# Attention's end of a four-layer graph network: its own order of work, softmax sums as a product, output norm regrouped

## The chip, the cores and the metric

One core of a Trainium2 chip runs the whole kernel. The metric is the device time of one execution in microseconds, as the median of several runs. Five engines work side by side and meet only at semaphores: TensorE (PE in the profile, with its weight loads as PEld), VectorE (DVE), ScalarE (ACT), GpSimd (POOL) and SyncE (SP), which here only issues DMAs. Each engine takes its own instructions strictly in order.

## What is computed

A stack of four graph layers over x, 16 x 512 nodes x 128 features, each followed by a residual and a layer norm. Only the last layer and its norm matter here:

```python
# layer 3, per image; h = 4 heads of 32, E = 256 edges
e = einsum(leaky_relu(Xq[src] + Xq[dst], 0.2), a) + log(A0[src, dst] + EPS)
m = segment_max(e, src)
ex = exp(e - m[src])
denom = segment_sum(ex, src)
attn = ex / denom[src]
Y = segment_sum(attn * Xv[dst], src)          # scatter
out = Y @ W_out.T
x = layernorm(x + out)                        # mean, variance over 128 features, eps 1e-5
```

## The kernel before

Everything stays in SBUF as X, [128, 4 chunks, 16 images, 128]. The edges were sorted by source at the start, so an edge's segment is a run of neighbours. `phase_attention` is the last stage. It is one hand-written list, `order`, of items (kind, n); every engine walks this same list and executes the kinds that are its own. The list is `first_part()` followed by `slot(k)`, one slot for each image with the stages of several images interleaved (`AHEAD` 5, `BEHIND` 9), and then whatever output norms are left.

The items of image n, in the order in which an image needs them:

- `z` (ACT, L2218): normalize the batch-norm output; `T` (PE transposes L2138, then the DVE addition L2290 into X); `s3` (DVE, four row statistics, L548), `v3` (DVE, six small instructions L2300 to L2305), `p3` (POOL, power -0.5, L2399), `sh3` (DVE, L2313), `ap3` (scale and shift by 128 columns, partly DVE L2345, partly ACT L2246): third layer norm.
- `xs` (ACT L2226 and POOL, high and low part of X), `G` (PE L2147, gather; evacuated by ACT L2230), `U` (PE L2155 and L2158, evacuated by ACT), `lr` (DVE L2321), `W` (PE L2166, scores).
- softmax of four images g at once, in a tile [16 rows, 256 edges]: `sc` (DVE L2370), `mx` (two scans, L2325 and L2326), `df` (L2374), `ex` (ACT, Exp, L2234), `su` (two more scans for the sums, L2330 and L2331), `at` (PE transposes of the exponentials L2174 and of the sums L2177, then DVE reciprocal L2336 and product L2337 into aT).
- `va` (POOL, V times aT, L2407), `vh` (ACT, its high part, L2240), `vl` (its low part; POOL for n below 8, DVE from 8 on, L72), `S` (PE L2186, scatter, evacuated by ACT L2230), `P` (PE L2195, output product), `R` (DVE addition L2290).
- output norm: `s4`, `v4`, `p4`, `sh4` as above by the groups in `GROUPS4`, then `ap4` (two chunks on DVE, two on ACT), and a 256 KB store by SP (L2120) for each image.

PE results for DVE rotate through three PSUM banks (`dve_ring`), those for ACT through four (`act_ring`); `begin_dve` and `begin_act` wait for the bank to be free. The steady slots of late images run G, U, S, W and P of different images one behind another on PE. Softmax 3 (images 12 to 15) comes at slot 18, after all gathers.

An order entry is a wait too: an engine whose next item isn't ready doesn't go on to a later one.

Of the kernel before, what the change touches and what calls it, by code (L numbers as in the profile page):

```python
# [6 lines left out]
ALU = mybir.AluOpType  # L7
# [558 lines left out]
def take_over(nc, sh, later):  # L566
# [36 lines left out]
    sh.free_to = first  # L603
    sh.consts_at = first - 4096
    sh.hidden = room("hidden", [P, NB, J, N], offset=first)
# [1202 lines left out]
def phase_batchnorm(nc, sh, d):  # L1808
# [8 lines left out]
    with ExitStack() as ctx:  # L1817
# [15 lines left out]

        pf, pr, kf = sh.pf, sh.pr, sh.kf = tuple(kept(name, [R, NE]) for name in ("pf", "pr", "kf"))
        wide = sh.wide = kept("wide", [P, 2 * R - NH])
# [44 lines left out]
        def _(dve):  # L1880
# [37 lines left out]
            def edge_constants():  # L1918

                dve.wait_ge(S["wide0"], 1)  # L1920
                dve.wait_ge(S["acol_in"], 16)
                for h in range(NH):
                    rows = slice(h * DH, (h + 1) * DH)
                    dve.tensor_copy(wide[rows, R - NH + h:R - NH + h + 1], acol[rows, 0:1])
                link(dve.tensor_tensor(ne[:, 1:NE], ss[0:R, 0, 1:NE], ss[0:R, 0, 0:NE - 1], ALU.not_equal))
                dve.tensor_scalar(pf[:, 1:NE], ne[:, 1:NE], LOWEST, None, ALU.mult)
                dve.tensor_scalar(kf[:, 1:NE], ne[:, 1:NE], -1.0, 1.0, ALU.mult, ALU.add)
                dve.tensor_scalar(pr[:, 0:NE - 1], ne[:, 1:NE], LOWEST, None, ALU.mult)
                dve.memset(pf[:, 0:1], LOWEST)
                dve.memset(kf[:, 0:1], 0.0)  # L1930
                dve.memset(pr[:, NE - 1:NE], LOWEST)
# [22 lines left out]
def phase_attention(nc, sh, d, out):  # L1954
# [8 lines left out]
    with ExitStack() as ctx:  # L1963
        sb, sem = allocators(nc, ctx)
        GZ, GsT, WT, lg = sh.GZ, sh.GsT, sh.aWT, sh.lg
        pf, pr, kf, wide = sh.pf, sh.pr, sh.kf, sh.wide
        UV = sb("aUV", [P, NB, 2 * NE])
# [9 lines left out]
        s1 = sb("s1", [R, NQ, NE])  # L1977
        s2 = sb("s2", [R, NQ, NE])
        inverse = sb("inverse", [P, NQ, K * R])
        aT = sb("aT", [P, K, NB, NH])  # L1980
# [13 lines left out]
        GROUPS3 = [(0, 1), (1, 2), (2, 3)] + [(b, min(b + 2, NB)) for b in range(3, NB, 2)]  # L1994
        GROUPS4 = [(0, 4), (4, 8), (8, 12), (12, 14), (14, 16)]

# [6 lines left out]
        def slot(k):  # L2003

            t, m = k + AHEAD, k - BEHIND
            g, part = divmod(k - 6, QB)
            softmax = part if 0 <= g < NQ else None
            ready = [i for i, (b0, b1) in enumerate(GROUPS3) if b1 == t and k > 1] + [2] * (k == 0) + [3] * (k == 1)
            items = [("p3", i) for i in ready if i > 2]
# [12 lines left out]
            if 0 <= m + 1 < NB:  # L2022
                items += [("vl", m + 1)]
            if 0 <= m - 2 < NB:
                items += [("s4", m - 2)] + [("v4", i) for i, (b0, b1) in enumerate(GROUPS4) if b1 == m - 1]
# [6 lines left out]
            if 4 <= k + 2 < NB:  # L2032
                items += [("xs", k + 2)]
            if softmax == 0:
                items += [("ex", g)]
            if 0 <= k - 1 < NB:
                items += [("U", k - 1)]
            if softmax == 1:
                items += [("at", g)]
            items += [("sh3", i) for i in ready]  # L2040
# [5 lines left out]
            if t < NB:  # L2046
                items += [("s3", t)] + [("v3", i) for i, (b0, b1) in enumerate(GROUPS3) if b1 == t + 1]
            if softmax == 0:
                items += [("su", g)]
            if 0 <= m < NB:  # L2050
                items += [("S", m)]
            if 0 <= k - 2 < NB:
                items += [("W", k - 2)]
            if 0 <= m - 1 < NB:
                items += [("P", m - 1)]
            if 0 <= m + 2 < NB:
                items += [("va", m + 2)]
# [6 lines left out]
            return items  # L2064

        order = first_part()
        for k_ in range(NB + BEHIND + 5):
            order += slot(k_)
        for g_, (b0_, b1_) in enumerate(GROUPS4):
            order += [item for item in [("sh4", g_)] + [("ap4", b) for b in range(b0_, b1_)] if item not in order]  # L2070

        def chunks3(n):

            split = C // 2 if n < 3 else C - 1 if 5 < n < 11 else 1
            return range(0, split), range(split, C)

        def low_on_dve(n):

            return n >= NB - BEHIND + 1

        dve_ring, act_ring = {}, {}
        for item_ in order:
            if item_[0] in ("T", "at", "P"):
# [20 lines left out]
        def weighted_low(eng, n):  # L2104
            eng.wait_ge(S["va_hi"], n + 1)
            low_part(eng, val[:, n % QB, :, :], va[:, n % QB, :, :], vah[:, n % QB, :, :])\
                .then_inc(S["va_lo"], 1)
# [3 lines left out]
        @block.sync  # L2111
        def _(sp):
            ov = out.rearrange("b (c p) d -> p c b d", p=P)
            done = 0
            for item in order:
                if item[0] == "ap4":
                    n, done = item[1], done + 1
                    sp.wait_ge(S["x4_dve"], done)
                    sp.wait_ge(S["x4_act"], done)
                    sp.dma_start(ov[:, :, n, :], sh.X[:, :, n, :]).then_inc(S["stored"], 16)  # L2120
            sp.wait_ge(S["stored"], 16 * NB)

        @block.tensor
        def _(pe):
# [44 lines left out]
            def attention_turned(g):  # L2169
                to = dve_bank(("at", g))  # L2170
                pe.wait_ge(S["ex_done"], g + 1)
                begin_dve(("at", g))
                for k in range(K):
                    pe.transpose(to[:, k * R:(k + 1) * R], s2[:, g, k * P:(k + 1) * P], sh.ident[0:R, 0:R])  # L2174
                pe.wait_ge(S["soft"], 4 * (g + 1))
# [22 lines left out]
            for kind, n in order:  # L2198
# [6 lines left out]
                elif kind == "W":  # L2205
                    scores(n)
                elif kind == "at":
                    attention_turned(n)
                elif kind == "S":
                    scatter(n)  # L2210
                elif kind == "P":
                    project(n)

        @block.scalar
        def _(act):
# [34 lines left out]
            for item in order:  # L2250
# [17 lines left out]
                elif kind == "ap4":  # L2268
                    apply(n, 4, range(C // 2, C)).then_inc(S["x4_act"], 1)

        @block.vector
        def _(dve):
# [54 lines left out]

            def sums(g):
                dve.wait_ge(S["ex_done"], g + 1)
                then(dve.tensor_tensor_scan(s1[:, g, :], kf[:, :], s2[:, g, :], 0.0, ALU.mult, ALU.add))  # L2330
                then(dve.tensor_tensor_scan(sco[:, g, ::-1], pr[:, ::-1], s1[:, g, ::-1], 0.0, ALU.add, ALU.max))  # L2331

            def attention(g):
                tile = dve_bank(("at", g))
                dve.wait_ge(S["pe_dve"], dve_ring["at", g] + 1)
                link(dve.reciprocal(inverse[:, g, :], tile[:, K * R:2 * K * R]))  # L2336
                dve.tensor_tensor(aT[:, :, QB * g:QB * (g + 1), :],  # L2337
                                  tile[:, 0:K * R].rearrange("p (k b h) -> p k b h", k=K, b=QB),
                                  inverse[:, g, :].rearrange("p (k b h) -> p k b h", k=K, b=QB), ALU.mult)\
# [9 lines left out]
            for item in order:  # L2349
# [23 lines left out]
                elif kind == "df":  # L2373
                    dve.tensor_tensor(s1[:, n, :], sco[:, n, :], s2[:, n, :], ALU.subtract).then_inc(S["sd_done"], 1)  # L2374
                elif kind == "su":
                    sums(n)
                elif kind == "at":
                    attention(n)
# [8 lines left out]
                elif kind == "sh4":  # L2387
                    shifts(4, n, rows_of(GROUPS4, n))
                elif kind == "ap4":
                    dve.wait_ge(S["shift4"], group_of(GROUPS4, n) + 1)  # L2390
                    apply(n, 4, range(0, C // 2)).then_inc(S["x4_dve"], 1)

        @block.gpsimd
        def _(pool):
# [7 lines left out]
            def weighted(n):  # L2402
                pool.wait_ge(S["dve_free"], dve_ring["at", n // QB] + 1)
                if n >= QB:
# [89 lines left out]
```

## Time and profile before

| | |
|---|---|
| median of three runs | 1010.1 us (1010.0 to 1010.34) |
| profiled execution | 1015.05 us, span 1013.0 us |
| last stage, from the first z to the end | 873.7 to 1013.0 us |
| PE busy | 926.2 us, 91% |
| DVE busy | 671.9 us, 66% |
| ACT busy | 538.4 us, 53% |
| POOL busy | 309.3 us, 31% |
| mean granted TensorE clock | 0.969 |

The shares are averages over stages with different limits. The page's slices show DVE at eight and nine tenths in the last eighth of the span, where PE falls to five tenths at one place and to nothing at the end.

### The profile page before, as it was taken

What the parts mean: (1) busy time and instruction counts of PE and PEld (TensorE: products, weight loads), DVE (VectorE), ACT (ScalarE), POOL (GpSimd) and SP (SyncE); (2) the same over time, 40 slices, a digit from 0 to 9 for tenths busy, and PEclk for the clock granted to TensorE, in tenths of its full rate; (3) what the DMA queues carried; (4) which work ended last, traced back from release to release, by engine and by line L of the source; (5) the groups of instructions that cost most, each with busy time, mean ns of one, the idle gap of its engine ahead of it and who ended that gap; (6) DMA issues with size and microseconds to landing.
All of it is one profiled execution on the core that took longest, in us unless ns stands there. A gap on an engine that the chain in (4) does not pass through costs nothing. (4 is left out here: it accounts for less than half of the span.)

```text
span 1013.0 us, 14415 instructions
## 1 busy us (share of the span) xinstructions
PE 926.2 (91%) x5120; PEld 795.4 (79%) x5120; DVE 671.9 (66%) x1662; ACT 538.4 (53%) x1112; POOL 309.3 (31%) x284
## 2 busy tenths in 40 slices
PE   6999997999998999998999999899999978588984
PEld 4689986899997898997889899787788853365763
DVE  6665435445546657655755675697887876779887
ACT  2043324664645565554565564557567548366644
POOL 3011222332323233232323333314333220155742
PEclk9989999999999999999999999999979998799987
DMA  8030011001010100101010001201100000000014
GB/s 223 1 81 17 7 63 63 1 22 42 1 42 2 42 22 1 42 2 42 1 42 21 29 15 35 89 1 63 42 1 22 2 0 1 0 1 1 0 44 123
DMA packets 33995, 31.62 MB, mean 31 GB/s; under 512 B 8451, under 2 KB 28035, under 8 KB 33925
## 3 DMA queue, kind: packets, MB, share of 16 engines
q1 hardware_dynamic: 32900, 30.64, 9.9%
q8 instruction: 41, 0.67, 0.3%
q14 instruction: 30, 0.24, 0.1%
q10 hardware_dynamic: 960, 0.07, 0.1%
q0 software_dynamic: 64, 0.00, 0.0%
HBM read 22.83 MB, written 7.87 MB: 30 GB/s over the span
## 5 line engine op out<-in xcount | busy, mean ns | idle before, releaser
L1322 ACT ACTIVATE gates<-psum,gbias 128x256 f32<-128x256 f32 (+2 forms) x312 | 158.9, 566 | 68.5 <-PE psum L67 64.5
L65 PE MATMUL psum<-LS,WI 128*128 128x256 f32 (+2 forms) x312 | 105.0, 337 | 8.9 <-ACT gates L1322 5.3
L67 PE MATMUL psum<-LS,WI 128*128 128x256 f32 (+2 forms) x312 | 103.6, 332 | 0.0
L66 PE MATMUL psum<-LS,WI 128*128 128x256 f32 (+2 forms) x312 | 103.6, 332 | 0.0
L72 POOL TENSOR_TENSOR LS<-A,LS 128x512 fp32r<-128x512 f32 (+2 forms) x44 | 49.0, 1114 | 170.7 <-ACT LS L1307 170.6
L72 POOL TENSOR_TENSOR LS<-Hodd,LS 128x512 fp32r<-128x512 f32 (+2 forms) x44 | 48.6, 1103 | 150.4 <-ACT LS L1307 150.4
L72 DVE TENSOR_TENSOR yl<-psum,yh 128x512 fp32r<-128x512 f32 x58 | 39.6, 688 | 65.1 <-ACT yh L1264 44.0
L72 POOL TENSOR_TENSOR XSl<-X,XSh 128x512 fp32r<-128x512 f32 x32 | 42.6, 1334 | 115.9 <-ACT XSh L1259 115.9
L65 PEld LDWEIGHTS psum<-LS,WI 128*128 128x128 f32 x312 | 59.8, 192 | 18.2 <-POOL LS L72 9.9
L1329 ACT ACTIVATE tc<-cell 128x512 f32<-128x512 f32 (+2 forms) x88 | 45.3, 514 | 53.5 <-DVE cell L1617 29.4
L65 PE MATMUL psum<-B2h,LT2h 128*128 128x256 f32 x256 | 72.7, 284 | 1.0 <-DVE X L1435 1.0
L67 PE MATMUL psum<-B2h,LT2l 128*128 128x256 f32 x256 | 72.4, 283 | 0.0
L66 PE MATMUL psum<-B2l,LT2h 128*128 128x256 f32 x256 | 72.4, 283 | 0.0
L66 PEld LDWEIGHTS psum<-LS,WI 128*128 128x128 f32 x312 | 60.0, 192 | 5.0
L67 PEld LDWEIGHTS psum<-LS,WI 128*128 128x128 f32 x312 | 60.0, 192 | 4.2
L65 PE MATMUL psum<-LS,WH 128*128 128x256 f32 (+2 forms) x192 | 60.3, 314 | 0.0
L66 PE MATMUL psum<-LS,WH 128*128 128x256 f32 (+2 forms) x192 | 59.9, 312 | 0.0
L67 PE MATMUL psum<-LS,WH 128*128 128x256 f32 (+2 forms) x192 | 59.8, 312 | 0.0
L65 PE MATMUL psum<-Eh,yh 128*128 128x384 f32 x168 | 56.6, 337 | 0.0
L67 PE MATMUL psum<-Eh,yl 128*128 128x384 f32 x168 | 56.3, 335 | 0.0
L66 PE MATMUL psum<-El,yh 128*128 128x384 f32 x168 | 56.2, 335 | 0.0
L548 DVE BATCH_NORM_STATS2 nstats<-X 128x6 f32<-128x128 f32 x256 | 54.1, 277 | 0.4
(372 smaller groups left out, 2680.8 us busy)
## 6 DMA issues: line engine op xcount, KB each, us to landing
WI<-lstm_weights SPq DMA_DIRECT2D x14, 512.0 KB, 3.6
WH<-lstm_weights SPq DMA_DIRECT2D x11, 512.0 KB, 4.6
X<-in_x SPq DMA_DIRECT2D x16, 256.0 KB
out<-X SPq DMA_DIRECT2D x16, 256.0 KB, 2.3
lstm_weights<-WI SPq DMA_DIRECT2D x4, 512.0 KB, 2.6
lstm_weights<-WH SPq DMA_DIRECT2D x3, 512.0 KB, 2.7
A<-in_adj SPq DMA_DIRECT2D x4, 256.0 KB, 4.4
z_A<-in_adj SPq DMA_DIRECT2D x1, 1024.0 KB, 5.3
```

The source lines that it names most:

```text
L65: pe.matmul(out, lhs[0], rhs[0], start=start, stop=False)
L66: pe.matmul(out, lhs[0], rhs[1], start=False, stop=False)
L67: return pe.matmul(out, lhs[1], rhs[0], start=False, stop=stop)
L72: return eng.tensor_tensor(out, full, high.bitcast(F32), ALU.subtract)
L548: return dve.bn_stats(self.stats[:, bass.ds(self.sh.C * n + c, 1), :], self.sh.X[:, c, bass.ds(n, 1), :])
L1322: act.activation(gates[:, gate, 0:n], sh.psum[:, gate, 0:n], ACT.Tanh if gate == G else ACT.Sigmoid, bias=gbias[:, p_ - 1, gate:gate + 1]) ...
L1329: act.activation(tcs[:, 0:n], cell[:, s % 2, 0:n], ACT.Tanh).then_inc(S["tanh_done"], 1)
```

## The change

1. The order of the end. `drain()` returns a written-out list of the last items, which replaces them at the end of `order`. In it softmax 3 goes ahead of the statistics and norms, `S` 9 and 10 stand ahead of its transposes, and `P` 8 and 9 behind.
2. Softmax sums. The two scans of `su` and the transposes of their result are gone. A constant `same` [128, 2, 256], one where two edges have the same source, is made by two DVE instructions in the batch-norm phase (one of 16 rows, `kf`, and a memset go). `at` transposes only the exponentials; a new item `ec` (DVE) copies them out of PSUM to `exT`; a new item `dn` multiplies `same` by `exT` on PE (four fp32 matmuls of 16 columns), and its DVE part holds the reciprocal and the product into aT. `va` waits for `dn`. `dn` stands behind `S` and `W` in its slot, and takes a turn in the ring of three banks.
3. Groups of the output norm: seven in place of five, the last of one image.
4. Output norms: ACT has all four chunks up to image 9, three up to 13, two for 14 and 15. SP waits for DVE only where DVE has a part.
5. `vl` of images 8 to 11 goes from DVE to POOL.
6. `variances`, of both norms, has five instructions in place of six (the epsilon goes into an earlier one).

```diff
-        GROUPS4 = [(0, 4), (4, 8), (8, 12), (12, 14), (14, 16)]
+        GROUPS4 = [(0, 4), (4, 7), (7, 9), (9, 11), (11, 13), (13, 15), (15, 16)]
...
             if softmax == 1 and not closing:
-                items += [("at", g)]
+                items += [("at", g), ("ec", g)]
...
             if 0 <= k - 2 < NB:
                 items += [("W", k - 2)]
+            if softmax == 1 and not closing:
+                items += [("dn", g)]
             if 0 <= m - 1 < NB:
                 items += [("P", m - 1)]
...
+        def drain():
+
+            first = [("vh", 10), ("sc", 3), ("mx", 3), ("df", 3), ("S", 9), ("vl", 10), ("ex", 3), ("va", 11), ("S", 10),
+                     ("R", 7), ("at", 3), ("vh", 11), ("ec", 3), ("vl", 11), ("p4", 1), ("dn", 3), ("va", 12), ("ap4", 3)]
+            weighted = [("P", 8), ("P", 9), ("s4", 7), ("R", 8), ("sh4", 1), ("ap4", 4), ("vh", 12), ("S", 11), ("R", 9), ("vl", 12),
+                        ("va", 13), ("s4", 8), ("v4", 2), ("P", 10), ("p4", 2), ("S", 12), ("vh", 13), ("s4", 9), ("R", 10),
+                        ("vl", 13), ("va", 14), ("ap4", 5), ("P", 11), ("S", 13), ("vh", 14), ("s4", 10), ("R", 11),
+                        ("vl", 14), ("va", 15), ("v4", 3), ("p4", 3), ("P", 12), ("sh4", 2), ("ap4", 6), ("S", 14),
+                        ("vh", 15), ("s4", 11), ("R", 12), ("vl", 15)]
+            last = [("P", 13), ("ap4", 7), ("S", 15), ("s4", 12), ("v4", 4), ("p4", 4), ("R", 13), ("sh4", 3), ("ap4", 8),
+                    ("P", 14), ("s4", 13), ("ap4", 9), ("R", 14), ("P", 15), ("s4", 14), ("v4", 5), ("p4", 5), ("sh4", 4),
+                    ("R", 15), ("ap4", 10), ("s4", 15), ("v4", 6), ("p4", 6), ("ap4", 11), ("ap4", 12), ("sh4", 5),
+                    ("ap4", 13), ("ap4", 14), ("sh4", 6), ("ap4", 15)]
+            return first + weighted + last
...
+        closing = drain()
+        order = [item for item in order if item not in closing] + closing
...
+        def chunks4(n):
+
+            split = 0 if n < 10 else 1 if n < NB - 2 else C // 2
+            return range(0, split), range(split, C)
+
         def low_on_dve(n):
 
-            return n >= NB - BEHIND + 1
+            return n >= NB - QB
...
+            def denominators(g):
+                to = dve_bank(("dn", g))
+                pe.wait_ge(S["dve_free"], dve_ring["at", g] + 1)
+                begin_dve(("dn", g))
                 for k in range(K):
-                    ins = pe.transpose(to[:, (K + k) * R:(K + k + 1) * R], sco[:, g, k * P:(k + 1) * P],
-                                       sh.ident[0:R, 0:R])
+                    for j in range(K):
+                        ins = pe.matmul(to[:, k * R:(k + 1) * R], same[:, j, k * P:(k + 1) * P],
+                                        exT[:, g, j * R:(j + 1) * R], start=(j == 0), stop=(j == K - 1))
                 ins.then_inc(S["pe_dve"], 1)
...
-                dve.tensor_tensor(a, stats[:, :, 1], stats[:, :, 4], ALU.add)
-                dve.tensor_tensor(c, stats[:, :, 2], stats[:, :, 5], ALU.add)
-                link(dve.tensor_tensor(b, stats[:, :, 1], stats[:, :, 4], ALU.subtract))
+                dve.tensor_tensor(b, stats[:, :, 1], stats[:, :, 4], ALU.subtract)
+                dve.scalar_tensor_tensor(c, stats[:, :, 2], D * EPS, stats[:, :, 5], ALU.add, ALU.add)
+                link(dve.tensor_tensor(a, stats[:, :, 1], stats[:, :, 4], ALU.add))
                 link(dve.scalar_tensor_tensor(b, b, 0.25, b, ALU.mult, ALU.mult))
-                link(dve.scalar_tensor_tensor(b, c, 1.0 / D, b, ALU.mult, ALU.add))
-                return dve.tensor_scalar(b, b, EPS, None, ALU.add)
+                return dve.scalar_tensor_tensor(b, c, 1.0 / D, b, ALU.mult, ALU.add)
...
-            def sums(g):
-                dve.wait_ge(S["ex_done"], g + 1)
-                then(dve.tensor_tensor_scan(s1[:, g, :], kf[:, :], s2[:, g, :], 0.0, ALU.mult, ALU.add))
-                then(dve.tensor_tensor_scan(sco[:, g, ::-1], pr[:, ::-1], s1[:, g, ::-1], 0.0, ALU.add, ALU.max))
+            def exponentials_copied(g):
+                dve.wait_ge(S["pe_dve"], dve_ring["at", g] + 1)
+                dve.tensor_copy(exT[:, g, :], dve_bank(("at", g))[:, 0:K * R]).then_inc(S["dve_free"], 1)
```

## Rows read from the trace of the kernel before

**Rows 1.** Windows: length, busy (count) of PE PEld DVE ACT POOL, clock, DMA.

```profile
925.00:935.00 10.00, 9.29 (x41) 7.01 (x42) 8.96 (x28) 5.11 (x10) 6.10 (x9) 0.83 0.00 0
...
976.00:983.00 7.00, 3.02 (x23) 2.56 (x21) 6.69 (x22) 2.76 (x8) 1.47 (x1) 0.85 0.13 37
983.00:988.00 5.00, 5.00 (x18) 4.34 (x18) 4.48 (x15) 1.67 (x4) 4.08 (x8) 0.53 0.27 78
```

**Rows 2.** Chain that ended last, in order of time: start us, us, what.

```profile
878.08 0.17 DVE n3work L2305
878.25 0.60 DVE X L2290
```

**Rows 3.** Timeline (start, us, what) of DVE around the second batch-norm loop and softmax 0.

```profile
842.23 0.75 DVE L1913 TENSOR_SCALAR O<-psum,z_par 128x512 f32<-128x512 f32 x1 [2.90 <-PE psum L1860]
...
922.93 0.66 DVE L2330 TENSOR_TENSOR_SCAN s<-kf,s 16x256 f32<-16x256 f32 x1
...
926.18 0.34 DVE L2336 RECIPROCAL inverse<-psum 128x32 f32<-128x32 f32 x1
926.55 0.19 DVE L2337 TENSOR_TENSOR aT<-psum,inverse 128x32 f32<-128x32 f32 x1
...
932.04 1.28 DVE L2345 TENSOR_SCALAR X<-X,n3scale,n3shift 128x128 f32<-128x128 f32 x1
```

**Rows 4.** Timeline of ACT: high part and z after softmax 0, last output norms.

```profile
927.65 0.42 ACT L2240 ACTIVATE vah<-va 128x256 fp32r<-128x256 f32 x1 [3.11 <-POOL va L2407]
927.97 0.80 ACT L2218 ACTIVATE A<-O,bsh,bsc 128x512 f32<-128x512 f32 x1
...
1008.49 1.65 ACT L2246 ACTIVATE X<-X,n4shift,n4scale 128x128 f32<-128x128 f32 x4 [2.65 <-DVE n4shift L2313]
```

**Rows 5.** Timeline of PE around softmax 0, 1, 2 and 3.

```profile
924.36 0.29 PE L2177 MATMUL psum<-ident,sco 16*128 16x16 f32 x2 [2.26 <-DVE sco L2331]
...
929.76 0.60 PE L2138 MATMUL psum<-ident,A 128*128 128x128 f32 x4
...
946.06 0.29 PE L2177 MATMUL psum<-ident,sco 16*128 16x16 f32 x2 [0.62 <-DVE sco L2331]
...
967.70 0.27 PE L2177 MATMUL psum<-ident,sco 16*128 16x16 f32 x2
967.90 0.50 PE L2186 MATMUL psum<-z_GsT,vah 128*128 128x512 f32 x1
...
982.80 0.39 PE L2177 MATMUL psum<-ident,sco 16*128 16x16 f32 x2 [3.31 <-DVE sco L2331]
983.13 0.80 PE L2186 MATMUL psum<-z_GsT,vah 128*128 128x512 f32 x1
...
985.00 1.91 PE L2195 MATMUL psum<-z_aWT,aY 128*128 128x128 f32 x8
...
988.90 0.48 PE L2186 MATMUL psum<-z_GsT,vah 128*128 128x512 f32 x1
```

**Rows 6.** All waits of PE between 929.7 and 978: total, times, longest us.

```profile
PE psum L2177 <- DVE sco L2331: 0.6, 1, 0.6
```

**Rows 7.** One line's instructions, near the trace's start: duration min/median/max, first and last start.

```profile
L493 PE MATMUL psum<-icf,perm x8: 167/250/250, 32.1 to 32.8; 128*128 128x1 f32 x8
```

**Rows 8.** Timeline of POOL: a split, the powers, and va of the last images.

```profile
931.94 1.30 POOL L72 TENSOR_TENSOR aXL<-X,aXH 128x512 fp32r<-128x512 f32 x1
...
960.16 0.74 POOL L72 TENSOR_TENSOR val<-va,vah 128x256 fp32r<-128x256 f32 x1 [0.53 <-ACT vah L2240]
...
981.53 3.20 POOL L2399 TENSOR_TENSOR n4scale<-n4work,const 128x16 f32<-128x16 f32 x1 [9.76 <-DVE n4work L2305]
985.66 3.09 POOL L2407 TENSOR_TENSOR va<-aUV,aT 128x128 f32<-128x128 f32 x8 [0.92 <-DVE aT L2337]
...
1000.88 1.66 POOL L2399 TENSOR_TENSOR n4scale<-n4work,const 128x8 f32<-128x8 f32 x1 [3.40 <-DVE n4work L2305]
```

**Rows 9.** Timeline of DVE at softmax 3.

```profile
976.42 0.40 DVE L2370 TENSOR_TENSOR sco<-psum,lg 16x256 f32<-16x256 f32 x1
```

More of the change, by code:

```diff
@@ L603, in take_over @@
     sh.free_to = first
-    sh.consts_at = first - 4096
+    sh.consts_at = first - 5120
     sh.hidden = room("hidden", [P, NB, J, N], offset=first)
@@ L1832, in kept @@
             return t
-        pf, pr, kf = sh.pf, sh.pr, sh.kf = tuple(kept(name, [R, NE]) for name in ("pf", "pr", "kf"))
+        pf, pr = sh.pf, sh.pr = tuple(kept(name, [R, NE]) for name in ("pf", "pr"))
+        same = sh.same = kept("same", [P, NE // P, NE])
         wide = sh.wide = kept("wide", [P, 2 * R - NH])
@@ L1924, in edge_constants @@
                     dve.tensor_copy(wide[rows, R - NH + h:R - NH + h + 1], acol[rows, 0:1])
+                for k in range(NE // P):
+                    dve.tensor_scalar(same[:, k, :], ss[:, 0, :], sh.sc[:, k:k + 1], None, ALU.is_equal)
                 link(dve.tensor_tensor(ne[:, 1:NE], ss[0:R, 0, 1:NE], ss[0:R, 0, 0:NE - 1], ALU.not_equal))
                 dve.tensor_scalar(pf[:, 1:NE], ne[:, 1:NE], LOWEST, None, ALU.mult)
-                dve.tensor_scalar(kf[:, 1:NE], ne[:, 1:NE], -1.0, 1.0, ALU.mult, ALU.add)
                 dve.tensor_scalar(pr[:, 0:NE - 1], ne[:, 1:NE], LOWEST, None, ALU.mult)
                 dve.memset(pf[:, 0:1], LOWEST)
-                dve.memset(kf[:, 0:1], 0.0)
                 dve.memset(pr[:, NE - 1:NE], LOWEST)
@@ L1965, in phase_attention @@
         GZ, GsT, WT, lg = sh.GZ, sh.GsT, sh.aWT, sh.lg
-        pf, pr, kf, wide = sh.pf, sh.pr, sh.kf, sh.wide
+        pf, pr, same, wide = sh.pf, sh.pr, sh.same, sh.wide
         UV = sb("aUV", [P, NB, 2 * NE])
@@ L1978, in phase_attention @@
         s2 = sb("s2", [R, NQ, NE])
+        exT = sb("exT", [P, NQ, K * R])
         inverse = sb("inverse", [P, NQ, K * R])
@@ L2007, in slot @@
             softmax = part if 0 <= g < NQ else None
+            closing = False
             ready = [i for i, (b0, b1) in enumerate(GROUPS3) if b1 == t and k > 1] + [2] * (k == 0) + [3] * (k == 1)
@@ L2023, in slot @@
                 items += [("vl", m + 1)]
+            if softmax == 0 and closing:
+                items += [("ex", g)]
             if 0 <= m - 2 < NB:
@@ L2033, in slot @@
                 items += [("xs", k + 2)]
-            if softmax == 0:
+            if softmax == 0 and not closing:
                 items += [("ex", g)]
@@ L2037, in slot @@
                 items += [("U", k - 1)]
-            if softmax == 1:
-                items += [("at", g)]
+            if softmax == 1 and not closing:
+                items += [("at", g), ("ec", g)]
             items += [("sh3", i) for i in ready]
@@ L2047, in slot @@
                 items += [("s3", t)] + [("v3", i) for i, (b0, b1) in enumerate(GROUPS3) if b1 == t + 1]
-            if softmax == 0:
-                items += [("su", g)]
             if 0 <= m < NB:
@@ L2053, in slot @@
                 items += [("W", k - 2)]
+            if softmax == 1 and not closing:
+                items += [("dn", g)]
             if 0 <= m - 1 < NB:
                 items += [("P", m - 1)]
+            if softmax == 0 and closing:
+                items += [("at", g), ("ec", g), ("dn", g)]
             if 0 <= m + 2 < NB:
@@ L2064, in slot @@
             return items
+        def drain():
+            first = [("vh", 10), ("sc", 3), ("mx", 3), ("df", 3), ("S", 9), ("vl", 10), ("ex", 3), ("va", 11), ("S", 10),
+                     ("R", 7), ("at", 3), ("vh", 11), ("ec", 3), ("vl", 11), ("p4", 1), ("dn", 3), ("va", 12), ("ap4", 3)]
+            weighted = [("P", 8), ("P", 9), ("s4", 7), ("R", 8), ("sh4", 1), ("ap4", 4), ("vh", 12), ("S", 11), ("R", 9), ("vl", 12),
[4 rows of a table added]
+            last = [("P", 13), ("ap4", 7), ("S", 15), ("s4", 12), ("v4", 4), ("p4", 4), ("R", 13), ("sh4", 3), ("ap4", 8),
[3 rows of a table added]
+            return first + weighted + last
         order = first_part()
-        for k_ in range(NB + BEHIND + 5):
+        for k_ in range(NB + 2):
             order += slot(k_)
-        for g_, (b0_, b1_) in enumerate(GROUPS4):
-            order += [item for item in [("sh4", g_)] + [("ap4", b) for b in range(b0_, b1_)] if item not in order]
+        closing = drain()
+        order = [item for item in order if item not in closing] + closing
         def chunks3(n):
@@ L2075, in chunks3 @@
             return range(0, split), range(split, C)
+        def chunks4(n):
+            split = 0 if n < 10 else 1 if n < NB - 2 else C // 2
+            return range(0, split), range(split, C)
         def low_on_dve(n):
-            return n >= NB - BEHIND + 1
+            return n >= NB - QB
         dve_ring, act_ring = {}, {}
         for item_ in order:
-            if item_[0] in ("T", "at", "P"):
+            if item_[0] in ("T", "at", "dn", "P"):
                 dve_ring[item_] = len(dve_ring)
@@ L2105, in weighted_low @@
             eng.wait_ge(S["va_hi"], n + 1)
+            if n and low_on_dve(n) != low_on_dve(n - 1):
+                eng.wait_ge(S["va_lo"], n)
             low_part(eng, val[:, n % QB, :, :], va[:, n % QB, :, :], vah[:, n % QB, :, :])\
@@ L2113, in _ @@
             ov = out.rearrange("b (c p) d -> p c b d", p=P)
-            done = 0
+            done = halved = 0
             for item in order:
                 if item[0] == "ap4":
-                    n, done = item[1], done + 1
-                    sp.wait_ge(S["x4_dve"], done)
+                    n = item[1]
+                    done, halved = done + 1, halved + (len(chunks4(n)[0]) > 0)
+                    if chunks4(n)[0]:
+                        sp.wait_ge(S["x4_dve"], halved)
                     sp.wait_ge(S["x4_act"], done)
@@ L2208, in _ @@
                     attention_turned(n)
+                elif kind == "dn":
+                    denominators(n)
                 elif kind == "S":
@@ L2268, in _ @@
                 elif kind == "ap4":
-                    apply(n, 4, range(C // 2, C)).then_inc(S["x4_act"], 1)
+                    apply(n, 4, chunks4(n)[1]).then_inc(S["x4_act"], 1)
         @block.vector
@@ L2326, in maximum @@
                 then(dve.tensor_tensor_scan(s2[:, g, ::-1], pr[:, ::-1], s1[:, g, ::-1], LOWEST, ALU.add, ALU.max))
-            def sums(g):
-                dve.wait_ge(S["ex_done"], g + 1)
-                then(dve.tensor_tensor_scan(s1[:, g, :], kf[:, :], s2[:, g, :], 0.0, ALU.mult, ALU.add))
-                then(dve.tensor_tensor_scan(sco[:, g, ::-1], pr[:, ::-1], s1[:, g, ::-1], 0.0, ALU.add, ALU.max))
+            def exponentials_copied(g):
+                dve.wait_ge(S["pe_dve"], dve_ring["at", g] + 1)
+                dve.tensor_copy(exT[:, g, :], dve_bank(("at", g))[:, 0:K * R]).then_inc(S["dve_free"], 1)
             def attention(g):
-                tile = dve_bank(("at", g))
-                dve.wait_ge(S["pe_dve"], dve_ring["at", g] + 1)
-                link(dve.reciprocal(inverse[:, g, :], tile[:, K * R:2 * K * R]))
+                dve.wait_ge(S["pe_dve"], dve_ring["dn", g] + 1)
+                link(dve.reciprocal(inverse[:, g, :], dve_bank(("dn", g))[:, 0:K * R]))
                 dve.tensor_tensor(aT[:, :, QB * g:QB * (g + 1), :],
-                                  tile[:, 0:K * R].rearrange("p (k b h) -> p k b h", k=K, b=QB),
+                                  exT[:, g, :].rearrange("p (k b h) -> p k b h", k=K, b=QB),
                                   inverse[:, g, :].rearrange("p (k b h) -> p k b h", k=K, b=QB), ALU.mult)\
@@ L2374, in _ @@
                     dve.tensor_tensor(s1[:, n, :], sco[:, n, :], s2[:, n, :], ALU.subtract).then_inc(S["sd_done"], 1)
-                elif kind == "su":
-                    sums(n)
-                elif kind == "at":
+                elif kind == "ec":
+                    exponentials_copied(n)
+                elif kind == "dn":
                     attention(n)
@@ L2388, in _ @@
                     shifts(4, n, rows_of(GROUPS4, n))
-                elif kind == "ap4":
+                elif kind == "ap4" and chunks4(n)[0]:
                     dve.wait_ge(S["shift4"], group_of(GROUPS4, n) + 1)
-                    apply(n, 4, range(0, C // 2)).then_inc(S["x4_dve"], 1)
+                    apply(n, 4, chunks4(n)[0]).then_inc(S["x4_dve"], 1)
         @block.gpsimd
@@ L2402, in weighted @@
             def weighted(n):
-                pool.wait_ge(S["dve_free"], dve_ring["at", n // QB] + 1)
+                pool.wait_ge(S["dve_free"], dve_ring["dn", n // QB] + 1)
                 if n >= QB:
```

4 lines of the change are left out of this document (2 added, 2 removed).

## Prediction

> **What bounds the kernel now.** The change touches only the last stage and a few instructions ahead of it, so the first view is the windows over the end. PE is busy 9.29 of 10 us from 925 on, but at a granted clock of 0.83; from 976 to 983 it has 3.02 us of work in 7, and then it is busy in full from 983 to 988 at 0.53, nearly the lower level [rows 1]. The stage has three parts with different limits, and the rest of the views are read for each.
>
> Up to about 930 the chain of work goes from engine to engine, DVE above all: images' statistics, the six variance instructions, the power on POOL. From 929.7 to 978 PE's whole list of waits is one wait of 0.6 us, for the sums of softmax 1 [rows 6]: there PE is the bound, and DVE, ACT and POOL have slack. From 978 it is a latency chain: last scores, softmax 3, its transposes, aT, va on POOL, vh, vl, scatter, product, addition, statistics, power, norm, store. PE waits 3.31 us there for the two scans of the sums [rows 5], and POOL waits 0.92 us for aT before the last four va [rows 8]. The last norm chunks end at 1010.14 (1008.49 + 1.65) [rows 4], and the last store ends with the span at 1013.0, 2.86 us behind.
>
> **The change part by part.** I work in the trace's own time and move its last event; the span's change is then taken from the median.
>
> *Batch-norm phase.* Two DVE instructions of 128 x 256 for `same` against one of 16 rows and a memset. DVE then waits 2.90 us for PE ahead of its first evacuation [rows 3], far more than two of some 0.3 us each. Nothing; were the cover gone it would be 0.4.
>
> *Variances.* The sixth instruction goes. It holds its successor up by 0.17 to 0.20 us (878.08, next at 878.25) [rows 2]. In the chain up to 916 five variances of the third norm are in series with everything behind (877, 880, 893, 907, 916). 5 x 0.2 = **-1.0**. Those under PE's cover and in the end are in the walk below.
>
> *Softmax 0, at 922.* The two scans (1.4 us from 922.93) go, and PE no longer waits 2.26 us at 924.36 [rows 3, 5]. That looks like a gain but is not carried on. aT of image 0 now comes from DVE's `dn` item, which stands behind the copy, three norm chunks, statistics and variances: after the scans' place, `lr` 0.35, T 0.6, copy 0.2, chunks until 925.75 (they start beside a POOL split), statistics 0.8, variances 0.75, reciprocal 0.34 and product 0.19, so 927.85 against 926.74 before [rows 3]. ACT stands at vh(0) until va is there: 927.65 now, 928.7 then; z(13) follows, 0.8 later, and PE's T(13) that starts at 929.76 needs it [rows 4, 5]: 928.7 + 0.35 + 0.75 = 929.8. Same place. So **0**; if aT isn't late, -1.0.
>
 Both groups: -0.6 - 2 x 0.2 + 2 x 0.8 = **+0.6** for PE's queue; laid out item by item it is +0.45, as a queue that doesn't stop saves a further 0.15 of restart, and the walk below starts from that. DVE now stands at `dn` until PE is there (967.8 to 970.05 for group 2) with lr(14), R(5) and sh4(0) queued behind it; W(14) wants lr(14) at 972.9 only, so that is covered by 1.7 us.
>
> A page speaks against item 5: the Trainium skill, "SBUF — State Buffer", section on the two separate sides, says that VectorE with two SBUF inputs and GpSimd exclude each other for a whole instruction. The trace agrees: a norm chunk of 0.34 took 1.28 us from 932.04 on, beside a POOL split that ran from 931.94 for 1.30 [rows 3, 8]. By that, four more products on POOL of 0.74 us each [rows 8] could hold DVE for 3 us; I count none of it, because DVE has shed two scans and its norm chunks where they run (968 to 982).
>
> *The end, walked.* P(5) is at 970.0, W(15) ends at 976.0. ACT takes 1.65 us for four chunks [rows 4], vl on POOL 0.74 [rows 8]. S(9) runs 976.9 to 977.9. DVE has R(6), s4(6), v4(1) ahead of the scores, so `sc` is at 976.7 against 976.42 [rows 9]; df ends 978.95; Exp 979.0 to 979.4; S(10), ahead of the transposes, waits for vl(10) and runs 979.0 to 980.0; `at` 980.15; copy 980.4; `dn` 981.2; aT 981.85. Before, the sums came at 982.8 and aT at 985.6 [rows 5, 8], so softmax 3 is 3.7 us earlier. Of that POOL takes back 2.3: p4(1) stands ahead of va(12) and behind vl(11), which isn't ready until 981.05 and ends 981.8; the power of 12 columns takes 2.4 us (16 take 3.20, 8 take 1.66 [rows 8]), so va(12) starts at 984.2 against 985.66 [rows 8]. sh4(1) at 984.3 lets ACT do ap4(4) to 986.0 and only then vh(12), 986.4; vl(12) 986.8; S(12) 986.85, against 988.90 before [rows 5]. From there two queues run side by side. DVE: s4(8), v4, s4(9), R(10) to 989.75, vl(13), S(13) on PE 990.15, and so on; R(15) ends 1001.6, s4(15) 1002.7, v4(6) 1003.4, last shift 1005.1, its two chunks 1005.65. ACT: S(13) evacuated 991.8, S(14) 994.35, S(15) 997.0, and behind it the norms of 8 and 9 (3.2), of 10, 11 and 12 (3.6), a wait of 0.3 for sh4(5), those of 13 (1.2), 14 and 15 (1.6): **1006.9**. The 24 chunks of 32 that DVE gave up are ACT's now, and ACT ends last, by 1.2 us.
>
> Sum: 1006.9 - 1010.14 = -3.2; variances of the stage's start -1.0; together -4.2 us. Store behind the last chunk as before, 2.86. Span 1008.8, the profiled execution 1010.9; the median stood 5 below that execution, 1010.1 - 4.2 = **1005.9 us**.
>
> **The rivals.**
> *A, a low clock after 927.* PE now has its gap behind G(8), about 926.8 to 929.8, 3 us; a gap of 3.31 us at 979.5 was followed by half clock until 987.6 (S(10) took 1.87 us from 983.13 to 985.00, about twice its usual time) [rows 1, 5], and a gap of 2.26 plus 1.05 by half clock from 926 to 929. Then T(13), U(7), W(6), G(9) run at 1.2 GHz, 3.2 us where 1.6 would do, and in front of a PE-bound stretch: +1.6, **1007.5**.
> *B, the walk is too slow.* aT(0) isn't late (-1.0), `dn` costs 0.56 (-0.25 twice on the way): **1004.3**.
> *C, POOL and the order of the end eat softmax 3's gain.* If vl(11) or p4(1) is 2 us later, S(12) stands at 988.9 as before, and ACT's backlog moves with it: +2.1, **1008.0**, which is no change. Against it speak the 9.76 us POOL was idle ahead of its power [rows 8].
> *D, the end at half clock.* This is the one on the other side. Spread over latency gaps, PE may not get its clock back from `dn`(3) on. Then `dn`, P(8), P(9), S(11), P(10) take 8.6 us from 980.4 and S(12) is 3.0 later; three more images each cost 0.9: +5.7. With A, +7.3: **1013.2**, slower. It decides from about 6.2 us lost against the forecast, that is only if the low level holds for nearly all of 981 to 1000. Against it: PE's longest gap in the walk behind `dn` is 1.9 us, shorter than the 3.31 and the 2.26 that stood ahead of low clock. D without A gives **1011.6**, no change.
>
> **How the numbers follow.** Forecast 0.43, with 1004.5 to 1007 of its own. A 0.15, B 0.15, C 0.13, D alone 0.05, D with A 0.09. Faster by over 0.2% (about what a measurement can tell, 2.0 us, so below 1008.1): forecast, A and B, 0.73. Within: C and D alone, 0.18. Slower 0.09. The range takes B with a bit below it (1002.6) and C with the unknown costs of `dn` and the port above it (1009.5); left out are D's 0.14 and some 0.04 below.
>
> **What would show it.** No idle of PE for the sums; `dn` at 0.8 us for its eight passes; va(0) about 1 us late and T(13) in its old place; aT(3) near 981 and va(12) behind a power of 2.4 us; ACT without a gap from S(15) on and last to end, DVE some 1 us ahead. A granted clock under 1 in 929 to 932 shows A, in 982 to 998 D. The prediction is wrong if DVE and not ACT ends last by more than 1 us, or if va(12) starts before 982.

## The result and the profile after

The changed kernel takes 1007.26 us in the median against 1011.29 us of the kernel before, measured side by side. The medians lie 4.0 us apart; the ratio of the runs is 0.9947, 95% interval 0.9935 to 0.996, which is 5.4 us less. The forecast was 1005.9 us, 4.2 us less than the 1010.1 us known then, ratio 0.9958. The profiled executions have spans of 1013.0 and 1005.2 us, 7.8 apart, and 2.5 us of that lie ahead of the last stage: the first DVE addition of T is at 875.70 before and at 873.17 after. Of those, 2.3 are there at the last cell product of the LSTM (797.9 and 795.6), in code that the change doesn't touch. So spans of single executions can't be compared to a microsecond, and I measure inside the last stage.

Two lengths are used below. *The stage* runs from the first DVE addition of T to the end of the span: 137.30 us before, 132.03 after. *The tail* runs from the fifth such addition, T(4), to the end: 124.03 before, **119.07** after. The tail is the sharper one. Kernels whose code is the same up to T(4) differ there by 0.5 us (12.96 and 12.43 us from T(0)), while the same kernel twice gave tails of 118.21 and 118.29. The change is worth 4.96 us in the tail and 0.31 in the first four images, and the 0.31 is less than the 0.5 by which that stretch differs with the same code. Of every kernel but one there is a single profile, so a tail is one measurement.

The page of the kernel after, its head:

```profile
span 1005.2 us, 14453 instructions
PE 922.8 (92%) x5144; PEld 792.2 (79%) x5144; DVE 658.7 (66%) x1627; ACT 546.1 (54%) x1136; POOL 311.8 (31%) x290
PEclk9989999999999999999999999999999998889998
```

DVE has 13 us less work, ACT 8 more. In the clock row the slice before the last, where softmax 3 lies, has a 9 (the kernel before has an 8 there), and the last an 8 (a 7 before). The end in windows (length, busy of PE, PEld, DVE, ACT, POOL, granted clock, DMA):

```profile
917.00:927.00 10.00, 8.62 (x50) 6.61 (x49) 8.19 (x30) 5.65 (x12) 4.00 (x5) 1.00 0.00 1
...
976.00:984.00 8.00, 6.53 (x47) 6.01 (x48) 5.13 (x22) 4.84 (x14) 4.57 (x7) 1.00 0.23 66
984.00:990.00 6.00, 4.25 (x27) 3.51 (x25) 5.19 (x22) 4.95 (x14) 4.07 (x6) 1.00 0.15 44
990.00:996.00 6.00, 3.27 (x23) 2.71 (x21) 5.64 (x28) 5.79 (x16) 2.09 (x2) 1.00 0.45 130
996.00:1005.20 9.20, 0.00 (x0) 0.00 (x0) 4.54 (x22) 5.95 (x16) 2.68 (x2) 0.64 0.70 201
```

Where [rows 1] had 0.83 and 0.53, there is 1.00, until PE's work is over. PE's timeline at softmax 0 and 1, kernel after (start, us, what, idle before and its releaser), to be held against [rows 5]:

```profile
918.34 0.29 PE L2204 MATMUL psum<-ident,s 16*128 16x16 f32 x2
919.92 0.61 PE L2196 MATMUL psum<-lr,wide 128*16 128x256 f32 x2 [1.28 <-DVE lr L2358]
920.62 1.07 PE L2213 MATMUL psum<-exT,same 128*128 128x16 f32 x8
921.53 0.48 PE L2177 MATMUL psum<-z_GZ,aXH 128*128 128x512 f32 x1
...
923.46 0.60 PE L2168 MATMUL psum<-ident,A 128*128 128x128 f32 x4
...
941.74 1.06 PE L2213 MATMUL psum<-exT,same 128*128 128x16 f32 x8 [0.66 <-DVE exT L2367]
942.66 1.14 PE L2231 MATMUL psum<-z_aWT,aY 128*128 128x128 f32 x8
```

The product takes 0.91 us of PE (920.62 to 921.53, 941.74 to 942.66). The gather behind it runs at 0.23 a matmul, not at 0.43. And DVE, ACT and POOL at the end:

```profile
977.26 0.36 DVE L2371 RECIPROCAL inverse<-psum 128x32 f32<-128x32 f32 x1 [1.16 <-PE psum L2213]
977.65 0.19 DVE L2372 TENSOR_TENSOR aT<-exT,inverse 128x32 f32<-128x32 f32 x1
...
1000.12 0.60 DVE L2380 TENSOR_SCALAR X<-X,n4scale,n4shift 128x128 f32<-128x128 f32 x2
```

```profile
979.77 1.65 ACT L2284 ACTIVATE X<-X,n4shift,n4scale 128x128 f32<-128x128 f32 x4 [1.92 <-DVE n4shift L2350]
...
992.51 9.44 ACT L2284 ACTIVATE X<-X,n4shift,n4scale 128x128 f32<-128x128 f32 x24
```

```profile
977.08 2.27 POOL L2434 TENSOR_TENSOR n4scale<-n4work,const 128x12 f32<-128x12 f32 x1
979.31 1.47 POOL L2442 TENSOR_TENSOR va<-aUV,aT 128x128 f32<-128x128 f32 x4
```

ACT does its last 24 chunks without a gap and ends at 1001.95, DVE at 1000.72; the forecast had ACT last by 1.2 us, and it is 1.2. POOL's power of 12 columns stands in front of va(12), as the forecast had it.

### The profile page after: what moved, and what is told of

Read it like the earlier page. It is cut to its first block and busy times, and to the rows that moved or that the text cites. A ratio compares the mean times of both kernels' runs of the same rounds, so it can differ in the third digit from the quotient of the medians.

```text
span 1005.2 us, 14453 instructions
## 1 busy us (share of the span) xinstructions
PE 922.8 (92%) x5144; PEld 792.2 (79%) x5144; DVE 658.7 (66%) x1627; ACT 546.1 (54%) x1136; POOL 311.8 (31%) x290
## 5 line engine op out<-in xcount | busy, mean ns | idle before, releaser
L65 PEld LDWEIGHTS psum<-LS,WI 128*128 128x128 f32 x312 | 59.2, 190 | 19.5 <-POOL LS L72 10.2
L66 PEld LDWEIGHTS psum<-LS,WI 128*128 128x128 f32 x312 | 59.2, 190 | 5.0
L67 PEld LDWEIGHTS psum<-LS,WI 128*128 128x128 f32 x312 | 59.3, 190 | 4.2
```

The lines of the kernel that those rows point to most:

```text
L65: pe.matmul(out, lhs[0], rhs[0], start=start, stop=False)
L66: pe.matmul(out, lhs[0], rhs[1], start=False, stop=False)
L67: return pe.matmul(out, lhs[1], rhs[0], start=False, stop=stop)
```

## The experiments

Each run's tail is compared with that of the kernel that its text names first. The theory after reading the two traces: the variances give 0.2 us a group; the product takes PE's waits for the scans away and with them two stretches of low clock, and gives part of that back as PE work; the rest is the order of the end. Rivals: that the product brings nothing outside the end (my own prediction), and that groups and ScalarE's share carry the end, not the order.

**The variances alone.** The kernel before, with

```diff
-                link(dve.scalar_tensor_tensor(b, c, 1.0 / D, b, ALU.mult, ALU.add))
-                return dve.tensor_scalar(b, b, EPS, None, ALU.add)
+                return dve.scalar_tensor_tensor(b, c, 1.0 / D, b, ALU.mult, ALU.add)
```

and the epsilon in the line that sums the squares, as in the change.

> The kernel before with five instructions in the variances in place of six, nothing else. Measured by the length of the last stage, from the first DVE addition of T to the end of the span (137.3 us before, 132.0 after the change), which leaves out the earlier stages. As predicted: five variances of the third norm are in series, 0.2 us each, so sc(0) comes 1.0 us earlier in the stage and the stage is 136.2. Rival: PE's later bound and POOL's port absorb it; sc(0) 1.0 earlier but stage 137.0 or more.

1008.82 us against 1012.34, ratio 0.9969 (0.9951 to 0.9986). Stage 135.00; tail 122.58, **1.45 less**. sc(0) is 0.63 earlier counted from T(4), the same 0.6 in all kernels with it. But aT(1) is 1.06 earlier and the end 1.45: it doesn't stop at the fifth group, as the prediction had it, since DVE's chain sets aT(1) too. More than either theory said.

**The clock kept up.** The kernel before, with work for PE while it waits:

```diff
+                for _ in range(KEPT[g]):          # (8, 0, 0, 12)
+                    pe.matmul(to[:, 128:256], WT[:, 0, :], WT[:, 1, :], start=True, stop=True)
                 pe.wait_ge(S["soft"], 4 * (g + 1))
```

> The kernel before with fp32 products of constants (8 for softmax 0, 12 for softmax 3, into unused columns) put on PE while it waits for the sums. It asks how much of the gain at softmax 0 and 3 is the granted clock. Clock theory: the granted clock stays at 1.00 from 924 to 931 and from 980 to 990, G(8) takes 1.9 us in place of 3.5, T(13) comes 1.5 us earlier in the stage, S(10) takes 1.0 in place of 1.9; stage 134 to 135. Rival (as the prediction had it: T(13) waits for ACT's vh(0) and z): T(13) in its old place, and the stage shorter only at its end, 136 or more.

T(13) came 1.56 us earlier, so it did not wait for ACT: the prediction's reason for its 0 is refuted. The clock was 1.00 from 923 to 927 and from 975 to 990, as expected. But the gain is gone one softmax on. PE, ahead of DVE now, waits 1.95 us for the sums of softmax 1, and pays for that wait with low clock:

```profile
942.01 0.29 PE L2180 MATMUL psum<-ident,sco 16*128 16x16 f32 x2 [1.95 <-DVE sco L2334]
...
942.57 0.57 PE L2189 MATMUL psum<-z_GsT,val 128*128 128x512 f32 x1
942.94 0.63 PE L2189 MATMUL psum<-z_GsT,vah 128*128 128x512 f32 x1
...
944.89 1.70 PE L2198 MATMUL psum<-z_aWT,aY 128*128 128x128 f32 x8
946.34 0.48 PE L2148 MATMUL psum<-z_GZ,aXH 128*128 128x512 f32 x1
```

```profile
943.00:946.00 3.00, 3.00 (x10) 1.51 (x9) 2.20 (x10) 1.24 (x3) 2.31 (x4) 0.50 0.00 0
```

aT(1) stands where it stood (59.30 and 59.29 us from T(4)), sc(2) is 1.56 later, the end takes 0.6 of that back: stage 138.21 where 134 to 135 was expected, tail 124.98, 0.95 more; the ratio of the timed runs, 1.0013 (0.999 to 1.0036), tells nothing from no change. The clock kept up brings nothing by itself here: what PE gains has to be met by DVE.

**The product alone.** The kernel before with `same`, `exT`, `ec` and `dn`, and nothing else of the change.

> The kernel before with the sums by a TensorE product (same, exT, ec, dn) and nothing else of the change: old order of the end, old groups, norms half and half, six instructions. Theory: at softmax 0 T(13) comes 2.8 us earlier (no wait for scans, clock stays high), groups 1 and 2 give back 0.9 each for dn less 0.6 for the wait, softmax 3 gains the scans less dn and keeps the clock; stage 133 to 134.5. Rival (the prediction's term of 0 at softmax 0): T(13) in place, PE's queue +0.45 later, stage 136 to 137.

Neither came out: the stage is 137.91. T(13) is 1.70 us earlier from T(4), not 2.8, since the clock did not stay up:

```profile
919.32 0.61 PE L2182 MATMUL psum<-lr,wide 128*16 128x256 f32 x2 [1.28 <-DVE lr L2345]
920.02 1.07 PE L2199 MATMUL psum<-exT,same 128*128 128x16 f32 x8
...
924.01 1.05 PE L2154 MATMUL psum<-ident,A 128*128 128x128 f32 x4
```

From 921 to 925 the granted clock is 0.57. The changed kernel has the same wait of 1.28 and the same product, and 1.00 behind them. At the other end, sc(2) is 1.23 earlier, but the tail is 125.28, **1.25 more** than before; timed, 1.0011 (0.9985 to 1.0036), no difference that can be told. PE's longest wait from 916 on and two windows:

```profile
PE psum L2199 <- DVE exT L2354: 2.9, 1, 2.9
```

```profile
975.00:980.00 5.00, 1.87 (x9) 1.24 (x8) 4.24 (x20) 1.91 (x5) 2.86 (x1) 0.95 0.18 52
980.00:985.00 5.00, 5.00 (x20) 4.61 (x21) 3.24 (x11) 1.29 (x4) 3.11 (x9) 0.50 0.18 52
```

In the old order the copy of softmax 3 stands on DVE behind R(7), vl, s4, v4(1), norms, R(8), vl and s4, which begin at 974.24 and end at 979.20. PE waits 2.9 us for it, as it waited 3.31 for the scans, and gets the low clock again. At softmax 3 the product swaps a wait for a wait; there it needs the order.

**The scans in the new order.** The changed kernel with two scans per softmax again (`su` behind `df`, and both pairs of transposes in `at`).

> The changed kernel with the sums by two scans again, and the new order of the end kept (su(3) right behind df(3)). Theory: it loses what the product brought at softmax 0 (2.8) less what dn costs PE in groups 1 and 2 (1.2), and 0.5 to 1 at softmax 3: stage 134.5 to 135.5 (132.0 with the product). Rival: the product brings nothing outside the end: stage 132.5 or less.

Ratio 0.997 (0.995 to 0.999). Stage 132.76, but this profile has the short form of the first four images, so the tail tells: 120.36, 1.29 more than with the product. So the new end (order, groups, norms, low parts) takes 2.22 us off the variances' 122.58 even with scans, and **the product is worth 1.29 us in it**. That includes the clock: with scans it is 0.57 from 921 to 925 and 0.50 from 976 to 979, where the changed kernel has 1.00. Of T(13)'s 2.83 us, 0.63 are left at sc(3): 40.16 against 37.33, 86.92 against 86.29.

**The order taken back.** The changed kernel with `closing = drain()` and the two lines around it removed, and the slots run on to the end as before.

> The changed kernel with the order of the end taken back (softmax 3 and the norms in their old slots); product, groups, norms on ScalarE, products on POOL and variances stay. If the order is what makes the product pay at softmax 3: PE waits some 2.9 us for exT(3) as with the product alone, clock low behind it, aT(3) after 107 us of the stage (104.5 with the new order), stage 135 or more (132.0). Rival (groups and ScalarE's share carry the end): 133 or less.

The first came out. Tail 123.37, stage 136.33, **4.30 more**; aT(3) at 107.9 us of the stage. PE waits 1.9 us for exT(3) and 1.2 for the exponentials, then the clock is low:

```profile
PE psum L2199 <- DVE exT L2353: 1.9, 1, 1.9
PE psum L2190 <- ACT s L2258: 1.2, 1, 1.2
```

```profile
975.00:980.00 5.00, 2.54 (x11) 1.90 (x12) 3.74 (x17) 5.00 (x13) 2.17 (x5) 0.84 0.20 59
980.00:985.00 5.00, 5.00 (x21) 4.61 (x21) 2.42 (x9) 2.20 (x7) 3.51 (x8) 0.50 0.35 100
```

**Norms half and half.** `split = C // 2` for all images.

> The changed kernel with all output norms half on DVE and half on ACT again. If ACT's sum of work sets the end, ACT loses 24 chunks of 0.39 us and DVE, which ended 1.2 us ahead with some 2 us of waits behind 980, gets 24 of 0.26, 6.2 us: DVE ends last, stage 134 to 135. Rival (the latency chain of the last images sets the end): stage within 0.5 of 132.0.

Tail 120.56, 1.49 more, less than the expectation's 2 to 3, and ACT still ends last (117.24 us from T(4), DVE 116.64). The share that went to ACT is worth 1.5 us; that DVE would end last was wrong. The clock falls to 0.50 from 984 to 987 here, but that isn't the cause: S(15) starts at 117.11 us of the stage, 0.5 earlier than in the changed kernel.

**Low parts on DVE.** `return n >= NB - BEHIND + 1` as before.

> The changed kernel with the low parts of images 8 to 11 on DVE again. PE waits 1.0 us for POOL's low part at S(9) or S(10), so with them on DVE (0.33 in place of 0.74) S(10) and the transposes of softmax 3 come earlier, but DVE has them ahead of sc(3) and df(3): sum near zero, stage 131.5 to 132.5. Rival: POOL's port lock was costing DVE, stage 131 or less.

Neither: tail 121.24, **2.17 more**. In DVE's queue vl(10) stands behind sc, mx and df of softmax 3, and PE waits for it in front of S(10), behind which stand the transposes:

```profile
PE psum L2222 <- DVE val L72: 4.2, 4, 2.3
```

The prediction weighed a page of the Trainium skill here, "SBUF — State Buffer", its section on the two separate sides, by which VectorE and GpSimd can exclude each other for a whole instruction, and estimated from it up to 3 us. The chunk that it showed beside a split has one tensor input, so it isn't the case of two inputs that it named. The two traces show what the neighbour costs: beside POOL's low parts the variances ahead of softmax 3 take 1.13 us and its second scan 1.03 (971.29 to 972.42 and 973.58 in the changed kernel), without them 0.69 and 0.68. That is 0.8 us, and the queue counts for more: the move to POOL pays 2.2 us net. Part of this is the clock again, 0.53 from 976 to 983 in this run, behind the wait of 2.3 us.

**Softmax 2 by scans, the others by the product.** The changed kernel with `SCANNED = (2,)`, for which `su` and both pairs of transposes are used.

> The changed kernel with softmax 2's sums alone by scans, the others by the product. PE is the bound there and DVE has slack, so dn's 0.92 us less two transposes come off PE's queue: sc(3) and aT(3) 0.7 us earlier in the stage, stage 131.4. Rival: PE's queue isn't what sets sc(3) (S(9) and S(10) wait for POOL's low parts): aT(3) moves by less than 0.2.

> The kernel of the look at softmax 2's sums by scans (product for 0, 1 and 3), timed. Its stage was 130.7 us against 132.0: 0.8 of it from PE's queue at softmax 2, 0.5 from a stretch ahead of softmax 0 that differs between kernels without a cause in them. If both hold in unprofiled runs, 0.8 to 1.3 us below the changed kernel's 5.4 us gain: ratio to the kernel before 0.9935 to 0.9945.

Tail 118.21, and 118.29 in the second profile: **0.8 less than the changed kernel**. sc(3) is 0.78 earlier and stays so to the end. PE is the bound at softmax 2, as the waits of before said [rows 6]. So the product there costs time in the changed kernel. Timed it gives 1006.26 against 1012.33, ratio 0.9945 (0.9921 to 0.9969): better than the kernel before, and not to be told from the changed kernel's 0.9947 by timing. Its tail is the shortest of all kernels.

**The product twice.** `for k in [*range(K), *range(K)]` in `denominators`.

> The changed kernel with dn's eight passes issued twice. One dn takes 0.91 us of PE. If PE's queue is the bound in the groups 1 and 2 and the chain runs through dn(3): aT(2) 1.8 later and sc(3) 1.8 later, aT(3) 2.7 later, stage 134.5. Rival (PE has slack at one of them, or ACT's sum of work swallows the last): stage 133.5 or less.

Tail 123.69, 4.62 more for four times 0.9 us, so the first case and more; the rest lies in two falls of the clock. At softmax 0 one further 0.9 us moved T(13) by 2.17: the clock was 0.60 from 923 to 927, where the changed kernel had 1.00, and it was 0.66 from 980 to 985. How near that stretch is to the low clock can't be seen in the changed kernel's own trace.

**va(12) ahead of the power.** In `drain`, `("p4", 1)` behind `("va", 12)`, `("vh", 12)` ahead of `("ap4", 4)`, `("sh4", 1)` behind `("va", 13)`.

> The changed kernel with va(12) ahead of p4(1) on POOL, vh(12) ahead of ap4(4) on ACT, and sh4(1) behind va(13). The prediction held that POOL's power in front of va(12) takes back 2 us of softmax 3's gain. If so, va(12) starts 1.4 us earlier and S(12) 2 us or more earlier, but ACT, which ends last, loses the gap it now has before ap4(4): stage 131.0 to 131.5. Rival (ACT's sum of work alone sets the end): S(12) earlier, stage 131.8 to 132.2.

The rival. Tail 118.96, 0.11 less. S(12) starts 1.6 us earlier (988.31 in that profile, 107.5 us of the stage against 109.1), and S(13), whose va now waits for the power, gets the gap: PE waits 1.9 us there and the clock falls to 0.75 in 990 to 995. Softmax 3's gain isn't held up by the power in front of va(12); what isn't lost there is lost an image on.

**Two more chunks for DVE.** `split` 1 for images 10 and 11 only, 2 from 12 on.

> The changed kernel with two chunks of the output norms of images 12 and 13 on DVE in place of one. ACT ends last by 1.2 us; two chunks of 0.39 us leave it and 0.52 us goes to DVE, so both end near 128.0 and the stage is 131.3. Rival: chunks aren't in the tail's chain, the end is set by the last group's power and shift: no change.

Tail 118.99, 0.08 less, so the rival. ACT's waits behind 985 show why: 

```profile
ACT X L2284 <- DVE n4shift L2350: 0.6, 1, 0.6
```

That wait isn't there in the changed kernel. ACT has fewer chunks and waits for a shift of DVE instead, so both engines bind at the end.

## Why the prediction was right, and where it wasn't

Moments in us of the stage, from the first addition of T. The forecast's are its own times less 1.0 for the variances and 875.7 for the stage's start.

| | before | forecast | after |
|---|---|---|---|
| T(13) starts on PE | 54.06 | 53.1 | 50.29 |
| P(5) starts | 93.87 | 93.3 | 91.89 |
| sc(3) starts | 100.72 | 100.0 | 99.25 |
| aT(3) done | 109.88 | 105.15 | 104.67 |
| va(12) starts | 109.96 | 107.5 | 106.14 |
| S(12) starts | 113.20 | 110.15 | 109.06 |
| DVE's last chunk ends | 133.91 | 128.95 | 127.55 |
| ACT's last chunk ends | 134.44 | 130.2 | 128.78 |
| end of span | 137.30 | 133.1 | 132.03 |

The direction, the size and the tail's shape came out. The walk of the end holds: from sc(3) to aT(3) done 5.15 forecast, 5.42 measured; from aT(3) to ACT's last chunk 25.05 and 24.11.

*Variances, -1.0.* At sc(0) it is that: 0.94 in the changed kernel, 0.63 of it behind T(4) and 0.31 in the stretch that differs by 0.5 without a cause. Under PE's cover I gave it nothing, and the run with them alone shows 1.06 at aT(1) and 1.45 of the tail, with 0.3 in front of T(4): some 1.75 in all. The term was under-sized by some 0.75, because DVE still sets softmax 1 although PE's list of waits shows only 0.6 us for it.

*Softmax 0, 0.* This step failed. It rested on T(13) needing the z behind vh(0). That z is image 14's; image 13's had run one slot earlier. In the trace after, T(13) starts at 923.46 and the z behind vh(0) at 925.51. T(13) waited for PE alone, for its gap and for the 1.6 us that the low clock cost in G(8) (3.5 us before, 1.9 after). Less the variances' 0.94, it came 2.83 us earlier. It was named as rival B, at -1.0 and by another way. How much of the 2.83 is sure is another question. The seven other profiles with the product at softmax 0, issued once, and the shorter variances have T(13) within 0.05 us of the changed kernel, counted from T(4). The product alone, with the same waits there, got the low clock and came only 1.70 earlier. What decides between them isn't shown.

*Softmax 1 and 2, +0.6.* dn measured 0.91, not 0.8: 0.2 more for two. The output product, which the prediction took for an upper bound of 1.1, also takes 0.91 from its start to the next instruction's (941.33 to 942.24 before), so its 0.136 a pass isn't what the trace shows. The wait of 0.62 for the sums became one of 0.66 for exT [rows 5], since the copy stands on DVE behind s4(0): not seen. From T(13) to P(5) the forecast took 40.2, and it took 41.60, so 1.4 of softmax 0's 2.8 was lost here, and the forecast's P(5) was off by only the other 1.4. That two steps missed in opposite ways is part of why the sum was near.

*The order, and what it depends on.* The prediction saw 3.7 us at aT(3) as the product's and the order's together and didn't say that the one needs the other. Product alone +1.25, the order taken away +4.30: at softmax 3 the product pays only where DVE's copy has nothing in front of it. So the parts can't be added up. The whole new end is worth 2.22 us with scans, while from the changed kernel the order alone, ScalarE's share alone and POOL's low parts alone cost 4.30, 1.49 and 2.17 when they are taken out.

*POOL takes back 2.3.* The power does stand before va(12), 2.27 us long, but the run with va(12) first moved the end by 0.11. It was no loss to the end. This is where the prediction's own sign of being wrong stands, va(12) before 982. In the walk's time, which leaves the variances' 1.0 out, va(12) starts at 982.8; with them it is 981.8. So it is at the edge, because the power started 1.2 us earlier than walked. The other sign, DVE last, didn't come: ACT is last by 1.2.

*Rivals.* A, low clock behind 927: not there; clock 1.00, and PE's gap behind G(8) didn't come about, as T(13) followed at once. C didn't occur. D, the end at half clock, didn't either; PE's longest wait behind softmax 3 is 1.32 us. But every run with a wait of 1.9 us or more shows it behind that wait (for instance 1.95 in the kernel with the clock kept up, 2.9 with the product alone, 1.9 with the old order and with va(12) first, 2.3 with low parts on DVE), and two show it near softmax 3 behind waits of 1.0 (norms half and half, the product twice). It came for a few microseconds at a time, not over the whole end as the rival had it.

What stays open: groups of the output norm were not tried apart from the rest; why the clock fell at softmax 0 with the product alone and not in the changed kernel; and the 0.5 us among the first four images, which comes and goes between kernels with the same code there.

## What to carry to other kernels

An engine that waits is also an engine whose clock may fall, but taking the wait away at one place sends it to the next meeting with the slower engine; look there before counting it. When a step is handed from one engine to another, put its hand-over items ahead of all other work in both queues, or the new wait replaces the old one. Where one engine's list of waits is nearly empty, still ask which engine sets the few waits that it has.

## What the runs showed of the hardware

In the last stage each wait of TensorE of about 1.9 us or more, in all these runs, was followed by the lower of its two clock levels, 0.50 of full speed, that is 1.2 GHz. The shortest are 1.87 us (va(12) first, clock 0.75 over 990 to 995), 1.91 (old order, 0.50 from 980 to 985) and 1.95 (kept up, 0.50 from 943 to 946). Shorter waits were followed by it in some runs and not in others. A wait of 1.28 us and a product of 0.91 behind it had 1.00 in the changed kernel and 0.57 over the next 4 us with the product alone; with one further 0.9 us product behind the same wait (1.29) it was 0.60. A wait of 1.02 us ahead of softmax 3 had 1.00 behind it in the changed kernel, and one of 1.01 had 0.50 from 984 to 987 with the norms half and half. So the length of the last wait alone doesn't tell it. All these are single profiles.

Four fp32 matmuls of 16 columns on 128-column weights take 0.91 us in eight passes, 0.114 a pass. The output product's eight passes with 128 columns take the same 0.91 (935.32 to 936.23 in the changed kernel), so with these weights an eighth of the columns saved nothing.

A dependent step in the variances costs DVE 0.20 us at 4 and 8 columns and 0.21 at 16, so larger groups save steps and smaller ones cost them.
